# GpSimd's indexed stores of edge messages: ahead of each pair of units, one more wait, on a matmul group two units further on

## The chip, the cores and the metric

The kernel runs on one core of a Trainium2 chip. The metric is the device time of one execution in microseconds (us), as the median of several runs. The core has five engines with in-order instruction streams: TensorE (PE; its weight loads are listed as PEld), VectorE (DVE), ScalarE (ACT), GpSimd (POOL) and SyncE (SP, which here only issues transfers). They meet through semaphores.

## The reference

One layer of a graph network, added to its input: 12,500 nodes with 128 features, 400,000 edges sorted by their target node `dst`.

```python
h = relu(layernorm(x))                                  # 12500 x 128
hW = h @ W_in2f.T
Wij = smu(edge_attr_20 @ W_f1.T + b_f1) @ W_f2.T + b_f2 # per edge, 20 -> 128 -> 128
Wij = Wij * edge_weight[:, None]
x_ij = hW[dst] * Wij                                    # gather, times filter
agg = segment_sum(x_ij, src, num_segments=12500)        # src is not sorted
out = x + smu(agg @ W_o1.T + b_o1) @ W_o2.T + b_o2
```

`smu(x) = ((1 + a) x + (1 - a) x erf(mu (1 - a) x)) / 2` with a = 0.01 and mu = 2.5. The kernel computes it as a gelu plus a linear part.

## The kernel before, in words

**Units, pairs, rounds.** The edges are padded to 401,408 and cut into 784 units of 512 edges (4 tiles of 128). Two units share one load of edge attributes, of targets and of a window of `hW` rows (a pair, `PAIR`). The 784 units form ten rounds of 112, 112, 112, 112, 80, 80, 56, 40, 40 and 40 units (`SIZES`). All engines run the same sequence of beats (`beats`, line 394), one beat for each unit; in each round some beats are written out and the rest run in a hardware loop of four beats. In beat c an engine works on unit c and on unit c - 1.

**What a unit n needs.** In the order of the data:

- PE `filter1` (line 1202) writes the first filter layer into the one bank `p_z`; ACT `gelu_of` (line 700) and DVE `smu` (line 975) make `act1` from it.
- DVE `pick_target` (line 979) makes a one-hot matrix of targets; PE `targets` (line 1219, 12 matmuls) gathers `hW[dst]` into `p_h`; ACT `weigh` (line 711) scales it into `hg`.
- PE `filter2` (line 1208, 4 matmuls in f32, which the profile counts as 8) adds the second filter layer to `p_w[v]`, v = n % 2, in which ACT has first put the bias (`add_to_bias`, line 725). Its last matmul increments the semaphore `s_w`, so `s_w` reads n + 1 once unit n has its filter.
- DVE `bucket_of`, PE `rank` (lines 1225 and 1241) and DVE `places` (line 999) work out to which row of a bucket of source nodes each edge goes; DVE `row_numbers` (line 1010) writes the row numbers to `row_idx`.
- DVE `message` (line 992) multiplies `p_w[v]` by `hg` into one of four slots of `msg` (`RING = 4`) and increments `s_msg`.
- ACT `keys` (line 704) adds one column to the slot.
- POOL `scatter` (line 575) stores the slot to DRAM (`sorted_rows`) by four indexed transfers of 128 rows of 516 bytes (line 581). They increment `s_scat[slot]` by 16 each when they have landed.

**Who waits for the stores.** `keys`, `row_numbers` and `message` of unit n wait until the stores of unit n - 4 have landed, since they write to the same slot. At the first bucket of each next round SP waits for all stores of the round (`load_buckets`, line 485). One round later the rows come back bucket by bucket (`seg`), and DVE `bucket_hot` (line 1025), PE `bucket_sum` (line 1253) and DVE `gather_sum` (lines 1036 and 1038) add them to `agg`. After the last round the same steps run for its buckets, and then 28 groups of nodes go through the two output layers.

**The order on the engines around the change.** The order is written out by hand, in the `step` function of each engine. PE in beat c does `filter1(c)`, `bucket_sum`, `rank(c-1)`, `targets(c-1)`, `filter2(c-1)`. DVE does `bucket_hot`, `smu(c)`, `pick_target(c)`, `bucket_of(c)`, `places(c-1)`, `gather_sum`, `row_numbers(c-1)`, `message(c-1)`. ACT does `gelu_of(c)`, `weigh(c-1)`, `keys(c-1)`, `limits(c)`, `add_to_bias(c)`. POOL does nothing but `scatter(c-1)` in its beats:

```python
wait_for(pool, s_idx, n, 1, 1)
wait_for(pool, s_key, n, 1, 1)
wait_for(pool, s_msg, n, 1, 1)
```

and after them the four stores. `wait_for(eng, sem, n, 1, k)` waits until the semaphore is at least n + k; in a loop n is worked out from the loop's register. The real edges end with unit 781, so POOL issues 3125 stores. After them POOL adds a bias to 28 groups of nodes (`add_bias`, line 600).

Of the kernel before, what the change touches and what calls it, by code (L numbers as in the profile page):

```python
# [11 lines left out]
TILES_U = 4  # L12
# [65 lines left out]
def wait_for(eng, sem, at, times=1, plus=0):  # L78
    v = at.value(times, plus)
    if at.i is None and v <= 0:  # L80
        return
    eng.wait_ge(sem, v)


def build(nc, n_nodes, n_edges, n_real, F, R, t):
    n_units = n_edges // UNIT
# [20 lines left out]
    real_tiles = -(-n_real // LANES)  # L107
# [25 lines left out]
    with ctx:  # L133
# [6 lines left out]
        def sem(name):  # L140
            return ctx.enter_context(nc.semaphore(name))
# [67 lines left out]
        with ExitStack() as ahead_only:  # L209
# [66 lines left out]
        s_z, s_gelu, s_smu, s_w, s_pick, s_ph, s_hg, s_msg, s_key = (  # L276
            sem(n) for n in ("s_z", "s_gelu", "s_smu", "s_w", "s_pick", "s_ph", "s_hg", "s_msg", "s_key"))
# [116 lines left out]
        def beats(eng, step, tail=True):  # L394
            for rnd in range(rounds):
                for c in range(BODY * peel(rnd)):
                    step(Beat(rnd, None, c))
                if peel(rnd) < SIZES[rnd] // BODY:
                    with eng.Fori(peel(rnd), SIZES[rnd] // BODY) as i:
                        for c in range(BODY):  # L400
                            step(Beat(rnd, i, c))
            for c in range(SEG_LAG + n_groups + TAIL_MORE if tail else 1):
                step(Beat(rounds, None, c))
# [7 lines left out]
        def if_general(eng, program):  # L411
            eng.wait_ge(s_flag, 1)
            anywhere = eng.value_load(general[0:1, 0:1], min_val=0, max_val=1)
            with eng.If(anywhere):
                program()
# [131 lines left out]
        @block.gpsimd  # L547
        def _(pool):
            pool.memset(w_f1[:, :], 0.0).then_inc(s_pool, 1)
            pool.memset(attr[:, :, :], 1.0).then_inc(s_attr_ones, 1)  # L550
            pool.memset(before[:, :], 1.0)
            pool.memset(not_before[:, :], 1.0)
            pool.memset(step_rows[:, :], float(SPACE))
            pool.iota(lane[:, :], pattern=[[0, 1]], base=0, channel_multiplier=1,
                      allow_small_or_imprecise_dtypes=True)
            pool.iota(iota[:, :], pattern=[[1, NODE_P]], base=0, channel_multiplier=0,
                      allow_small_or_imprecise_dtypes=True)
            pool.iota(iota_bf[:, :], pattern=[[1, BUCKETS]], base=0, channel_multiplier=0,
                      allow_small_or_imprecise_dtypes=True)
            pool.iota(win_limit[:, :], pattern=[[H_GROUP, n_pairs]], base=H_GROUP * (H_AHEAD - H_LAND) - WINDOW, channel_multiplier=0,  # L560
                      allow_small_or_imprecise_dtypes=True)
            pool.iota(seed_row[:, :, :], pattern=[[buf_rows // SPACE, BUFS], [1, BUCKETS]], base=0, channel_multiplier=0,
                      allow_small_or_imprecise_dtypes=True)
            pool.memset(ident[:, :], 0.0)
            pool.memset(ident_bf[:, :], 0.0).then_inc(s_pool, 1)
            pool.wait_ge(s_pool, 2)
            for m in (ident, ident_bf):
                pool.affine_select(out=m[:, :], in_=m[:, :], compare_op=ALU.not_equal, fill=1.0, base=0,
                                   pattern=[[-1, LANES]], channel_multiplier=1).then_inc(s_pool, 1)
            pool.affine_select(out=before[:, :], in_=before[:, :], compare_op=ALU.is_gt, fill=0.0, base=0,  # L570
                               pattern=[[1, LANES]], channel_multiplier=-1).then_inc(s_pool2, 1)
            pool.affine_select(out=not_before[:, :], in_=not_before[:, :], compare_op=ALU.is_ge, fill=0.0, base=0,
                               pattern=[[-1, LANES]], channel_multiplier=1).then_inc(s_pool2, 1)

            def scatter(n, slot, tiles=TILES_U):
                wait_for(pool, s_idx, n, 1, 1)
                wait_for(pool, s_key, n, 1, 1)
                wait_for(pool, s_msg, n, 1, 1)
                pool.sem_inc(s_go, 1)
                for k in range(tiles):  # L580
                    pool.indirect_dma_start(out=sorted_rows[:, :],  # L581
                                            out_offset=bass.IndirectOffsetOnAxis(ap=row_idx[:, slot, k:k + 1], axis=0),
                                            in_=msg[:, slot, k, :], in_offset=None).then_inc(s_scat[slot], 16)

            def step(st):
                if st.opens(1) and st.has(1):
                    if 0 < st.rnd_of(1) < BUFS:
                        pool.wait_ge(s_zero[st.rnd_of(1)], 16 * BUCKETS)
                    if st.rnd_of(1) >= BUFS:
                        pool.wait_ge(s_seg, first_item[st.rnd_of(1) - BUFS + 1])  # L590
                if st.i is None and st.rnd == 0 and st.c == mid_step:
                    pool.wait_ge(s_zero[0], 16 * BUCKETS)
                if st.has(1):
                    n = st.at(1)
                    scatter(n, st.ring(1), TILES_U if n.i is not None else max(0, min(TILES_U, real_tiles - n.base * TILES_U)))

            def add_bias(g, turn):
                deep, times = g % DEEP, turn * (n_groups // DEEP) + g // DEEP + 1
                pool.wait_ge(s_xl[deep], 48 * times)
                pool.tensor_tensor(x_out[:, deep, :, :], x_out[:, deep, :, :], bias_o2[:, :].unsqueeze(1).to_broadcast([NODE_P, NODE_G, F]),  # L600
                                   ALU.add).then_inc(s_xb, 1)

            beats(pool, step, tail=False)
            for g in range(n_groups):
                add_bias(g, 0)

            def everywhere():
                rows = seg[:, :, :, :].rearrange("p a b c -> p (a b c)").bitcast(BF16)[:, 0:TILES_U * PARTS * F].rearrange(
                    "p (k f) -> p k f", k=TILES_U)
                pool.wait_ge(s_seg, first_item[rounds])  # L610
                with pool.Fori(0, n_units) as u:
                    pool.wait_ge(g_ld, u * 32 + 32)
                    pool.sem_inc(s_go, 1)
                    for k in range(TILES_U):
                        pool.indirect_dma_start(out=rows[:, k, :], out_offset=None, in_=h3[:, :],
                                                in_offset=bass.IndirectOffsetOnAxis(ap=g_dst[:, k:k + 1], axis=0),
                                                ).then_inc(g_win, 16)

                for g in range(n_groups):
                    add_bias(g, 1)  # L620

            if_general(pool, everywhere)
# [776 lines left out]
```

## Time and profile before

| what | value |
|---|---|
| time before, median of 3 runs | 4107.2 us (4103.52 to 4111.21) |
| span of the profiled execution | 5749.3 us |
| PE busy | 4327.1 us (75%), 32406 matmul records |
| DVE busy | 3410.0 us (59%) |
| ACT busy | 2118.5 us (37%) |
| POOL busy | 3038.4 us (53%), of it 2997.9 us for the 3125 stores |
| mean granted TensorE clock | 0.833 of full speed |
| HBM traffic | 128 GB/s over the span |

The profiled execution has no time of its own in the result beside its span, and its span is 1642.1 us, or 40%, longer than the median of the runs without a profile. So absolute times of the trace, and idle times above all, can't be set equal to those of a timed run; a duration of one instruction, or the spacing of instructions that follow each other without a wait, is the safer reading. "Idle before" in the tables is time in which an engine had nothing in execution, put down to what ended it; "remote" is a semaphore update whose source the profile doesn't tell, and "issue" is time for which it shows no wait at all.

### The profile page before, as it was taken

How to read it: one execution, taken by the hardware profiler on the slowest of the kernel's cores; microseconds unless marked ns; L12 is line 12 of the kernel's file. 1: busy time of each engine (PE TensorE's matmuls, PEld its weight loads, DVE VectorE, ACT ScalarE, POOL GpSimd, SP SyncE). 2: the span in 40 equal slices, each digit the busy share in tenths (PEclk: the TensorE clock that was granted, in tenths of full speed). 3: DMA queues.
4: the chain of work that ended last, by engine and by line, in shares of the span. 5: the costliest groups of instructions: out<-in, count | busy, mean ns of one | idle time of the engine just before them, and what ended most of it. 6: DMA issues, size and time to landing. Idle time of an engine off the chain costs nothing. (4 is left out here: it accounts for less than half of the span.)

```text
span 5749.3 us, 112809 instructions
## 1 busy us (share of the span) xinstructions
PE 4327.1 (75%) x32406; PEld 3547.2 (62%) x32406; DVE 3410.0 (59%) x11848; ACT 2118.5 (37%) x7302; POOL 3038.4 (53%) x3173
## 2 busy tenths in 40 slices
PE   5666557777777777777777777777777887877778
PEld 4455446666666666666666666666666666666567
DVE  6555445555565555565555666665555666666667
ACT  3455333333333333333333333333333333333333
POOL 4555555555555555555555555555555555555553
PEclk7777777887787788887887888898888988888989
DMA  6354434444443443444443444444444445554446
GB/s 171 110 134 134 113 111 131 129 135 125 131 123 113 114 115 110 117 115 112 112 115 109 118 134 135 136 140 121 123 124 124 143 143 140 146 144 129 128 134 191
DMA packets 459438, 737.76 MB, mean 128 GB/s; under 512 B 87025, under 2 KB 255323, under 8 KB 458961
## 3 DMA queue, kind: packets, MB, share of 16 engines
q1 hardware_dynamic: 291462, 461.44, 30.7%
q0 software_dynamic: 100000, 206.60, 10.7%
q10 hardware_dynamic: 67626, 65.48, 3.5%
q8 instruction: 168, 2.75, 0.2%
q14 instruction: 182, 1.48, 0.1%
HBM read 465.36 MB, written 267.82 MB: 128 GB/s over the span
## 5 line engine op out<-in xcount | busy, mean ns | idle before, releaser
L581 POOL DMA_INDIRECT sorted_rows<-msg,row_idx x3125 | 2997.9, 959 | 2627.5 <-DVE msg L992 1739.1
L711 ACT ACTIVATE hg<-p_h,weight 128x128 f32<-128x128 f32 x3136 | 894.7, 370 | 3102.5 <-remote 2804.8
L1253 PEld LDWEIGHTS p_seg<-seg_hot,seg 128*128 128x128 f32 x8288 | 1206.5, 213 | 784.6 <-issue 781.9
L999 DVE CUSTOM_DVE_ANT_0 product<-onehot,p_pos,start_at 128x112 bf16<-128x112 bf16 x3136 | 846.0, 324 | 1392.8 <-remote 1356.7
L1253 PE MATMUL p_seg<-seg_hot,seg 128*128 128x112 f32 x8288 | 1275.6, 298 | 337.3 <-issue 318.7
L1208 PE MATMUL p_w<-w_f,act 128*128 128x128 f32 x6272 | 1144.1, 327 | 223.2 <-issue 215.2
L1208 PEld LDWEIGHTS p_w<-w_f,act 128*128 128x128 f32 x6272 | 983.2, 233 | 240.2 <-issue 237.9
L1202 PE MATMUL p_z<-attr,w_f 128*128 128x512 f32 x1568 | 985.9, 707 | 186.0 <-issue 110.9
L1219 PE MATMUL p_h<-win,pick 128*128 128x128 bf16 x9408 | 826.9, 250 | 293.3 <-ACT hg L711 210.9
L992 DVE TENSOR_TENSOR msg<-p_w,hg 128x512 f32<-128x512 f32 x784 | 539.0, 688 | 736.0 <-ACT hg L711 448.8
L1219 PEld LDWEIGHTS p_h<-win,pick 128*128 128x128 bf16 x9408 | 700.7, 114 | 326.1 <-issue 319.8
L700 ACT ACTIVATE gelu<-p_z 128x512 f32<-128x512 f32 x784 | 473.8, 604 | 420.2 <-PE p_z L1202 161.4
L975 DVE SCALAR_TENSOR_TENSOR act<-p_z,gelu 128x512 f32<-128x512 f32 x784 | 536.3, 684 | 150.8 <-issue 114.2
L1025 DVE SCALAR_TENSOR_TENSOR seg_hot<-seg,p_iota 128x560 f32<-128x560 f32 (+2 forms) x700 | 580.7, 835 | 4.3 <-DMA seg<-sorted_rows 3.5
L1225 PE MATMUL p_pos<-onehot,not_before 128*128 128x112 bf16 x3136 | 333.6, 233 | 284.7 <-DVE place L999 149.1
L1225 PEld LDWEIGHTS p_pos<-onehot,not_before 128*128 128x128 bf16 x3136 | 254.3, 110 | 450.6 <-issue 438.5
L984 DVE TENSOR_TENSOR onehot<-p_iota,node_l 128x448 bf16<-128x448 f32 x784 | 479.3, 611 | 0.0
L725 ACT COPY p_w<-bias_f 128x512 f32<-128x512 f32 x784 | 477.9, 610 | 0.0
L1202 PEld LDWEIGHTS p_z<-attr,w_f 128*128 128x128 f32 x1568 | 292.3, 225 | 274.7 <-issue 200.3
L1241 PE MATMUL p_pos<-onehot,before 128*128 128x112 bf16 x3136 | 337.4, 236 | 50.1 <-issue 49.9
L979 DVE TENSOR_SCALAR pick<-ends,win_row 128x512 bf16<-128x512 uint16 x784 | 300.1, 383 | 0.0
L1241 PEld LDWEIGHTS p_pos<-onehot,before 128*128 128x128 bf16 x3136 | 232.2, 111 | 64.3 <-issue 64.1
(110 smaller groups left out, 1715.7 us busy)
## 6 DMA issues: line engine op xcount, KB each, us to landing
seg<-sorted_rows SPq DMA_DIRECT2D x448, 322.5 KB
seg<-sorted_rows SPq DMA_DIRECT2D x196, 516.0 KB
ends<-ends SPq DMA_DIRECT2D x392, 256.0 KB
sorted_rows<-msg,row_idx POOLq DMA_INDIRECT x3125
sorted_rows<-zero_rows ACTq DMA_DIRECT2D x336, 129.0 KB
win<-h SPq DMA_DIRECT2D x392, 96.0 KB
attr<-in_attrT SPq DMA_DIRECT2D x392, 80.0 KB
seg<-sorted_rows SPq DMA_DIRECT2D x56, 387.0 KB
```

Source lines behind the costliest of these rows:

```text
L581: pool.indirect_dma_start(out=sorted_rows[:, :], out_offset=bass.IndirectOffsetOnAxis(ap=row_idx[:, slot, k:k + 1], axis=0), in_=msg[:, sl ...
L711: last = act.activation(hg[:, v, k, :], p_h[:, k, :], ACT.Copy, scale=weight[:, bass.ds(n.value(TILES_U, k), 1)])
L975: dve.scalar_tensor_tensor(act1[:, v, :], p_z[:, :], SMU_L, gelu[:, v, :], ALU.mult, ALU.add).then_inc(s_smu, 1)
L992: dve.tensor_tensor(msg[:, slot, :, 0:F], p_w[v][:, :, :], hg[:, v, :, :], ALU.mult).then_inc(s_msg, 1)
L999: last = dve.tensor_tensor_reduce(out=product[:, k, :], in0=onehot[:, slot, k, :], in1=p_pos[:, 0:BUCKETS], scale=1.0, scalar=start_at[:, ...
L1025: dve.scalar_tensor_tensor(seg_hot[:, it.slot, 0:n, :], seg[:, it.slot, 0:n, F:F + 1].to_broadcast([LANES, n, NODE_P]), -float(LANES * (it ...
L1202: pe.matmul(p_z[:, :], w_f1[:, :], attr[:, q, v * UNIT:(v + 1) * UNIT], start=True, stop=True).then_inc(s_z, 1)
L1208: last = pe.matmul(p_w[v][:, k, :], act1[:, v, k * LANES:(k + 1) * LANES], w_f2[:, :], start=False, stop=(k == TILES_U - 1), skip_group_ch ...
L1219: last = pe.matmul(p_h[:, k, :], pick[:, v, k * LANES:(k + 1) * LANES], win[:, q, part * F:(part + 1) * F], start=(part == 0), stop=(part ...
L1225: last = pe.matmul(p_pos[:, 0:BUCKETS], not_before[:, :], onehot[:, slot, k, :], start=False, stop=False, skip_group_check=True)
L1241: last = pe.matmul(p_pos[:, 0:BUCKETS], before[:, :], onehot[:, slot, k, :], start=False, stop=False, skip_group_check=True)
L1253: last = pe.matmul(out, seg[:, it.slot, l * it.tiles + k, 0:F], seg_hot[:, it.slot, l * it.tiles + k, :], start=(k == 0), stop=(k == it.ti ...
```

## The change

`scatter` gets one more argument, `opens_pair`. It is true where n is even (`st.v(1) == 0`), that is for the first unit of each pair n, n + 1. There POOL first waits until `s_w` is at least n + 3, which is the end of `filter2` of unit n + 2; near the end of the edges the number is cut to the number of units, 784. The stores, their order, the semaphores that they increment and all other engines stay as they are.

```diff
-            def scatter(n, slot, tiles=TILES_U):
+            def scatter(n, slot, opens_pair, tiles=TILES_U):
+                if opens_pair:
+                    if n.i is None:
+                        pool.wait_ge(s_w, min(n_units, n.base + 3))
+                    else:
+                        wait_for(pool, s_w, n, 1, 3)
                 wait_for(pool, s_idx, n, 1, 1)
                 wait_for(pool, s_key, n, 1, 1)
                 wait_for(pool, s_msg, n, 1, 1)
...
-                    scatter(n, st.ring(1), TILES_U if n.i is not None else max(0, min(TILES_U, real_tiles - n.base * TILES_U)))
+                    scatter(n, st.ring(1), st.v(1) == 0, TILES_U if n.i is not None else max(0, min(TILES_U, real_tiles - n.base * TILES_U)))
```

How it stands on POOL at the first four units, before (`s_msg`, `s_idx` and `s_key` are counts of finished messages, row numbers and keys):

```order
L581 DMA sorted_rows<-msg,row_idx 258048x129 [waits s_msg,s_idx,s_key]
L581 DMA sorted_rows<-msg,row_idx 258048x129 x3
L581 DMA sorted_rows<-msg,row_idx 258048x129 [waits s_msg,s_idx,s_key]
L581 DMA sorted_rows<-msg,row_idx 258048x129 x3
L581 DMA sorted_rows<-msg,row_idx 258048x129 [waits s_msg,s_idx,s_key]
L581 DMA sorted_rows<-msg,row_idx 258048x129 x3
```

and now, the same place:

```order
L586 DMA sorted_rows<-msg,row_idx 258048x129 [waits s_msg,s_key,s_w,s_idx]
L586 DMA sorted_rows<-msg,row_idx 258048x129 x3
L586 DMA sorted_rows<-msg,row_idx 258048x129 [waits s_msg,s_idx,s_key]
L586 DMA sorted_rows<-msg,row_idx 258048x129 x3
L586 DMA sorted_rows<-msg,row_idx 258048x129 [waits s_msg,s_key,s_w,s_idx]
L586 DMA sorted_rows<-msg,row_idx 258048x129 x3
```

Units 0 and 2 wait for `s_w` as well; unit 1 follows unit 0 with the waits that it had. No row has moved on any engine.

In the loop of a round POOL's four beats now read as follows (the loop begins with the second unit of a pair; `L82` is `wait_ge`, `L399` the loop):

```order
L586 DMA sorted_rows<-msg,row_idx 258048x129 [waits s_msg,s_idx,s_key]
L586 DMA sorted_rows<-msg,row_idx 258048x129 x3
L82 REGISTER_ALU
L82 REGISTER_ALU [waits s_w]
L586 DMA sorted_rows<-msg,row_idx 258048x129 [waits s_msg,s_idx,s_key]
L586 DMA sorted_rows<-msg,row_idx 258048x129 x3
L82 REGISTER_ALU
L586 DMA sorted_rows<-msg,row_idx 258048x129 [waits s_msg,s_idx,s_key]
L586 DMA sorted_rows<-msg,row_idx 258048x129 x3
L82 REGISTER_ALU
L586 DMA sorted_rows<-msg,row_idx 258048x129 [waits s_msg,s_key,s_w,s_idx]
L586 DMA sorted_rows<-msg,row_idx 258048x129 x3
```

The second and the fourth unit of the loop body are those that open a pair.

## Rows read from the trace of the kernel before

**Rows 1.** The page: span, busy time of each engine, and granted clock in 40 slices.

```profile
span 5749.3 us, 112809 instructions
...
PE 4327.1 (75%) x32406; PEld 3547.2 (62%) x32406; DVE 3410.0 (59%) x11848; ACT 2118.5 (37%) x7302; POOL 3038.4 (53%) x3173
...
PEclk7777777887787788887887888898888988888989
```

**Rows 2.** Line 581 by itself, the stores: min/median/max in ns, first and last start.

```profile
L581 POOL DMA_INDIRECT sorted_rows<-msg,row_idx x3125: 952/958/1222, 28.4 to 5630.4; - x196
```

**Rows 3.** Timeline of POOL, 3009 to 3024 us: start, length, instruction [idle before].

```profile
3009.46 0.96 POOL L581 DMA_INDIRECT sorted_rows<-msg,row_idx  x1 [2.67 <-DVE msg L992]
3010.72 0.95 POOL L581 DMA_INDIRECT sorted_rows<-msg,row_idx  x1 [0.30 <-issue]
...
3018.30 0.96 POOL L581 DMA_INDIRECT sorted_rows<-msg,row_idx  x1 [0.30 <-issue]
3023.80 0.96 POOL L581 DMA_INDIRECT sorted_rows<-msg,row_idx  x1 [4.54 <-DVE msg L992]
```

**Rows 4.** Waits: who waited for whom, us in total, times, longest us.

```profile
ACT hg L711 <- remote: 2804.8, 378, 12.0
POOL sorted_rows L581 <- DVE msg L992: 1739.1, 482, 5.7
DVE product L999 <- remote: 1356.7, 306, 8.8
```

**Rows 5.** Timeline of PE, the same stretch; the last rows lie behind a full burst of stores.

```profile
3009.98 1.13 PE L1202 MATMUL p_z<-attr,w_f 128*128 128x512 f32 x2 [0.86 <-DVE act L975]
...
3013.10 1.11 PE L1208 MATMUL p_w<-w_f,act 128*128 128x128 f32 x8
3014.05 1.06 PE L1202 MATMUL p_z<-attr,w_f 128*128 128x512 f32 x2
...
3017.95 0.38 PE L1253 MATMUL p_seg<-seg_hot,seg 128*128 128x112 f32 x2 [1.06 <-issue]
3019.38 0.25 PE L1225 MATMUL p_pos<-onehot,not_before 128*128 128x112 bf16 x1 [1.05 <-issue]
```

**Rows 6.** Timeline of ACT and DVE, the same stretch.

```profile
3009.42 0.23 ACT L704 ACTIVATE msg<-node_p 128x4 f32 x1
3009.80 0.62 ACT L725 COPY p_w<-bias_f 128x512 f32<-128x512 f32 x1
3021.03 1.14 ACT L711 ACTIVATE hg<-p_h,weight 128x128 f32<-128x128 f32 x4 [9.29 <-remote]
...
3007.86 0.69 DVE L992 TENSOR_TENSOR msg<-p_w,hg 128x512 f32<-128x512 f32 x1 [3.36 <-remote]
3012.01 0.68 DVE L992 TENSOR_TENSOR msg<-p_w,hg 128x512 f32<-128x512 f32 x1
```

**Rows 7.** Windows: busy us of each engine between two messages, and in early and late rounds.

```profile
core 0: us, PE busy (x) PEld busy (x) DVE busy (x) ACT busy (x) POOL busy (x), PEclk, DMA share, GB/s
3007.86:3012.01 4.15, 3.29 (x25) 2.62 (x24) 4.12 (x16) 3.08 (x10) 1.94 (x3) 1.00 0.42 119
...
800.00:1200.00 400.00, 291.88 (x2110) 240.27 (x2111) 227.16 (x806) 142.98 (x504) 211.77 (x222) 0.79 0.46 128
3200.00:3600.00 400.00, 312.63 (x2424) 260.13 (x2423) 246.12 (x858) 141.78 (x501) 216.03 (x226) 0.88 0.45 131
```

**Rows 8.** Timeline of the start: stores of units 0 and 1, message 0, filter2 of units 0 to 2.

```profile
28.41 1.12 POOL L581 DMA_INDIRECT sorted_rows<-msg,row_idx  x1 [22.44 <-issue]
35.76 0.96 POOL L581 DMA_INDIRECT sorted_rows<-msg,row_idx  x1 [2.43 <-DVE msg L992]
...
26.65 0.69 DVE L992 TENSOR_TENSOR msg<-p_w,hg 128x512 f32<-128x512 f32 x1 [3.03 <-ACT hg L711]
...
19.16 2.05 PE L1208 MATMUL p_w<-w_f,act 128*128 128x128 f32 x8 [4.14 <-DVE act L975]
32.63 1.13 PE L1208 MATMUL p_w<-w_f,act 128*128 128x128 f32 x8
36.41 1.11 PE L1208 MATMUL p_w<-w_f,act 128*128 128x128 f32 x8
```

## The prediction

> **What bounds the kernel now.** I read the page first. No engine looks full: PE is busy for 75% of the span, DVE for 59%, POOL for 53% [rows 1]. But this span is 5749.3 us and the runs take 4107.2, so I don't read idle time off it; I look for what can't be shorter in a run without a profile.
>
> The line of the stores gives 3125 of them at a median of 958 ns [rows 2]. The timeline of POOL shows what they cost: where nothing holds them, eight in a row start at 3009.46 to 3018.30, seven steps in 8.84 us, 1.263 us each, 0.96 busy and 0.30 between [rows 3]. So the stores alone take 3124 x 1.263 + 0.96 = 3946.6 us. Before the first lie 28.4 us, and behind the end of the last (5631.4) 117.9 us of last buckets and output layers [rows 1, 2]. The sum is **4092.9 us**, and the median run takes 4107.2: 14.3 us are left for all pauses of POOL. I conclude that in a timed run **GpSimd issues stores nearly without a pause**, 5.05 us for each unit, and that the other engines keep ahead of it.
>
> Can they? In an undisturbed stretch one message follows the other after 4.15 us (3007.86 to 3012.01), with DVE busy for 4.12 of it at full clock [rows 6, 7], and PE comes from one first layer to the next in 4.07 us (3009.98 to 3014.05) [rows 5]. Both are under 5.05. They are held by the ring: `keys`, `row_numbers` and `message` of unit n wait for the stores of unit n - 4.
>
> The profiled execution behaves otherwise. POOL waits 482 times for a message, 1739.1 us in all, ACT 378 times before `hg` and DVE 306 times before `product`, both for something the profile can't name [rows 4]. In the stretch shown PE's `targets` is over before 3013.3, its `filter2` begins at 3013.10, and yet ACT starts `hg` only at 3021.03, after 9.29 us of idleness; meanwhile PE creeps, with pauses of 1.05 us inside a group of matmuls that waits for nothing [rows 5, 6]. The release comes 1.77 us after the end of a burst of eight stores (3019.26) [rows 3]. Whatever that is, at this size it can't be in the timed runs, which have 14 us for it, as long as the spacing of the stores is the same there. (The Trainium skill, page "NOTIFIC — the notification-queue block", section 7.1, says that the block which writes trace records never drops one inside but holds up its producers. That would put the pauses down to the recording; no run here shows it.)
>
> **The change, part by part.** No instruction of work is added, removed or moved; 392 waits on `s_w` are added on POOL, one for each pair. In the loops each adds a register instruction, which POOL's sequencer runs while a store is in execution; I cost it at nothing, with the 0.96 us of a store as its cover, and at most one such instruction per pair if it is not covered.
>
> Behind the waiting instruction stand only the eight stores of its pair and those of later ones. For the stores wait: message, keys and row numbers four units later, SP at the first bucket of each round (eight units behind the round's last), and the tail. The wait itself is for `filter2` of unit n + 2, which needs nothing of the stores of n or n + 1, so it can't lock.
>
> *The start.* Message 0 ends at 27.34, and the first store starts at 28.41. `filter2` of unit 2 ends at 36.41 + 1.11 = 37.52 [rows 8]. So the first pair starts 10.2 us later. Since POOL is what the whole kernel waits for, what it loses before it runs full is not made up: this is 10.2 us at the end. If POOL is short of work for some units in a timed run too, the last moment at which it is short decides instead, and there the shift is what lies between message n and `filter2` of n + 2 with engines running free: from 3008.55 to 3014.21, 5.7 us [rows 5, 6]. I take 8, between the two, as the recording shows POOL short of work at its start (7.35 us from unit 0 to unit 1 against 5.05) [rows 8] but can't tell how long that lasts without a recording. Both ends go into the range.
>
> *The steady state.* `filter2` of n + 2 hangs on the bias of n + 2, which on ACT stands behind `keys` of n + 1, which waits for the stores of n - 3. The last of these starts nine steps before the pair n would, 11.4 us, and has landed at most 0.96 + 1.77 us later, 8.6 us before the pair. From `keys` to the end of the bias it is 3009.42 to 3010.42, 1.0 us [rows 6], then `filter2`, 1.11 [rows 5]. So the semaphore is there some **6.5 us before** POOL gets to the pair, if PE has done its earlier groups. The wait costs nothing as long as this reserve holds. Before the change only the message of n had to be there, which waits for the stores of n - 4: their last starts thirteen steps ahead, 16.4 us, less 2.7 for length and landing and 0.7 for the message [rows 3, 6], a reserve of 13.0. So the change halves the reserve of the one engine that must not pause.
>
> *The end.* The last stores come 8 us later, and the tail with them.
>
> Sum: 4107.2 + 8 = **4115 us**. The recorded span has its long pauses ahead of most bursts, and there the added wait lies beside the message that POOL waits for anyway; I expect it within 1.5% of 5749.
>
> One rule of the Trainium skill speaks to the spacing itself. The row first: beside a DVE that is busy for 4.12 of 4.15 us the stores keep their 0.96 us, and over all 3125 the shortest and the longest are 952 and 1222 ns [rows 2, 3, 7]. The page "SBUF — State Buffer", section "SBUF: two separate sides", says that a DVE instruction in a two-port mode locks GpSimd out, so that it can't write the descriptors of its transfers. By that, when the stores run would matter, and 3125 x 0.26 us = 0.8 ms would be the most at stake; the trace doesn't agree that it happens here, and the sum stays.
>
> **The rivals.**
>
> *A, the forecast: full POOL, wait covered but at the start.* +5.7 to +10.2 us, 4113 to 4117. Chance 0.40. A difference of 0.2% (8.2 us) is about what a measurement of this kernel can tell from none, so half of this case falls on either side.
>
> *B, the reserve doesn't hold: slower by more.* The place is POOL at the head of a pair while PE is at its lower clock. The mean granted clock is 0.79 of full speed at 800 to 1200 us and 0.88 later [rows 7]; with two levels, 1.2 and 2.4 GHz, that is 42% of the time at the lower. `filter2` took 2.05 us at the start and 1.11 later [rows 8], a ratio of 1.85, so a unit of PE takes some 7.5 us there instead of 4.07 and falls 2.5 us behind the stores. The 6.5 us are gone after 2.6 units; from then on POOL pauses. It decides from stretches at the lower clock of over some 20 us, or from any stall of PE over 6.5 us. If one pair in three loses 0.5 us, it is 65 us more: 4180. For it: PE is idle a fifth of the time behind a full POOL, and idleness is what went with a lower clock. Against it: a PE that lags has no idleness. Chance 0.26.
>
> *C, the pauses of the recording are real, and the change orders them: faster.* Then the stores are closer together in a timed run than 1.263 us. At the least, with no gap between them, they take 3125 x 0.96 = 3000 us, and 961 us are pauses. The recording has 482 pauses for 391 pairs; the change would leave one for each pair and let PE hand over `filter2` of two further units before each burst. With 91 of 482 gone, 961 x 0.19 = 181 us: 3926. With the spacing of the trace it can't gain over 14.3 us: 4093. For it: in the stretch shown everything is released just behind a burst's end. Against it: the sum that comes out within 0.4% with full stores. Chance 0.16.
>
> *D, the change does nothing.* If POOL is not what the end waits for, stores that are two units late land before the ring needs them: eight stores and the landing are 11.9 us, four units at 5.05 are 20.2. 4107. Chance 0.18.
>
> **The numbers.** The likeliest is A, 4115. The range takes in A, D, C as far as the trace's spacing allows it (4093, with some margin) and B to 65 us over A: 4087 to 4188; what is left out is the far end of C and a worse B, some 0.15. Slower: half of A and B, 0.46. Same: half of A and D, 0.38. Faster: C, 0.16.
>
> **What would show it.** In the changed profile the first store should start near 38.6 instead of 28.4. POOL's waits should name PE's `filter2`, line 1208 moved by five, in place of the message. Bursts should begin at even units only. The spacing should stay at 1.263 us, and the recorded span within 1.5%. I am wrong if a timed run is faster by over 14 us: then the stores were never 1.263 us apart without a recording, or POOL was not what bounds. I am wrong the other way if it is slower by over 12 us: then the reserve of 6.5 us is not there, and a version that waits for `filter2` of n + 1 should give most of it back.

## The result, and the profile after

The changed kernel takes **4127.25 us** in the median of four runs (4126.2 to 4134.98). Four runs of the kernel before on the same chip have a median of 4105.36 us (4101.37 to 4111.21). The ratio is 1.0055, with a 95% interval of 1.0043 to 1.0066: **slower by 22 us**, where 8 were forecast.

The page of the changed kernel. First the lines that answer to [rows 1], then its chain by engine, then the line of the stores:

```profile
span 4126.0 us, 112900 instructions
...
PE 3554.0 (86%) x32406; PEld 2965.5 (72%) x32406; DVE 3387.0 (82%) x11848; ACT 2149.7 (52%) x7302; POOL 3044.7 (74%) x3173
...
PEclk9999999999999999999999999999999999999989
...
POOL 35%; issue 22%; DMA 20%; PE 11%; DVE 8%; ACT 2%; POOLq 1%; ACTq 1%; SPq 0%; DVEq 0%
...
L586 POOL DMA_INDIRECT sorted_rows<-msg,row_idx x3125 | 3003.7, 961 | 1002.4 <-issue 868.7
```

The first thing to see is the span. The profiled execution itself took 4127.92 us, 1.9 us more than its span and 0.7 us more than the median. So recording costs nothing that shows in this run, and the 5749.3 us of [rows 1] can hardly be its doing. The clock was granted at 0.97 of full speed, against 0.833 there. What the difference is, the second and third groups of runs tell.

The waits of the changed kernel (who waited for whom: us in total, times, longest us):

```profile
ACT msg L709 <- DMA sorted_rows<-msg,row_idx: 1279.6, 629, 8.4
POOL sorted_rows L586 <- issue: 868.7, 2845, 0.8
DVE row_idx L1015 <- DMA sorted_rows<-msg,row_idx: 554.5, 405, 7.2
...
POOL sorted_rows L586 <- PE p_w L1213: 51.7, 111, 6.8
POOL sorted_rows L586 <- ACT msg L709: 41.2, 36, 30.5
```

This is the picture that the prediction drew from the sum alone. ACT's `keys` and DVE's `row_numbers` wait for stores to land, so both are ahead of POOL, and POOL waits for almost nothing: 2845 of its idle times are the ordinary 0.3 us between two stores. Of the 1739.1 us on a message in [rows 4] 22.9 are left, and "remote" is gone. New is the 51.7 us on `filter2`; most of its 111 times are the ordinary 0.3 us, only put down to it.

The timeline of POOL at the start, which answers to [rows 8] (units 0 and 1, then the first stores of unit 2):

```profile
36.46 1.12 POOL L586 DMA_INDIRECT sorted_rows<-msg,row_idx  x1 [30.49 <-ACT msg L709]
37.88 0.96 POOL L586 DMA_INDIRECT sorted_rows<-msg,row_idx  x1 [0.30 <-DVE row_idx L1015]
39.15 0.95 POOL L586 DMA_INDIRECT sorted_rows<-msg,row_idx  x1 [0.30 <-issue]
...
45.45 0.95 POOL L586 DMA_INDIRECT sorted_rows<-msg,row_idx  x1 [0.30 <-issue]
52.55 0.95 POOL L586 DMA_INDIRECT sorted_rows<-msg,row_idx  x1 [6.14 <-PE p_w L1213]
```

The first store starts 8.05 us later than in [rows 8] (in two later profiles of the kernel before it starts at 27.05 and 27.92). The spacing of the stores is as before: seven steps take 45.45 - 36.46 - 0.16 (the first is 1.12 long) = 8.83 us, 1.26 each. But the second pair stands still for 6.14 us. Over the whole run the starts of the 3125 stores leave 26.2 us above a steady spacing of 1.263, counting what is over 0.1 us, and 17.8 of these lie ahead of seven pairs, released by `filter2`: 5.8 us at unit 2, 0.7 at 4, 0.9 each at 66 and 110, 1.6 at 222, 1.35 at 334, 6.5 at 662. Units 110, 222, 334 and 662 are the last pairs of four rounds (rounds begin at 112, 224, 336 and 664).

### The profile page after: what moved, and what is told of

It reads as the page before. It is cut to its first block, busy times and chain, and to the rows that moved or that the text cites. A ratio compares the mean times of both kernels' runs of the same rounds, so it can differ in the third digit from the quotient of the medians.

```text
span 4126.0 us, 112900 instructions
## 1 busy us (share of the span) xinstructions
PE 3554.0 (86%) x32406; PEld 2965.5 (72%) x32406; DVE 3387.0 (82%) x11848; ACT 2149.7 (52%) x7302; POOL 3044.7 (74%) x3173
## 4 chain that ended last, share of the span: by engine, by line
POOL 35%; issue 22%; DMA 20%; PE 11%; DVE 8%; ACT 2%; POOLq 1%; ACTq 1%; SPq 0%; DVEq 0%
POOL sorted_rows L586 35%; DMA sorted_rows<-msg,row_idx 18%; PE p_seg L1258 4%; PE p_w L1213 3%; PE p_z L1207 2%; DVE product L1004 2%; DVE msg L997 1%; DVE seg_hot L1030 1%; PE p_h L1224 1%; DVE act L980 1%; DVE onehot L989 1%; DVE pick L984 1%; ACT p_w L730 1%; PE p_w L1268 1%; DVE row_idx L1015 0%
## 5 line engine op out<-in xcount | busy, mean ns | idle before, releaser
L1258 PEld LDWEIGHTS p_seg<-seg_hot,seg 128*128 128x128 f32 x8288 | 1055.5, 196 | 330.6 <-issue 328.8
L1213 PE MATMUL p_w<-w_f,act 128*128 128x128 f32 x6272 | 902.6, 288 | 352.6 <-ACT p_w L730 345.4
L1213 PEld LDWEIGHTS p_w<-w_f,act 128*128 128x128 f32 x6272 | 783.1, 196 | 403.8 <-issue 401.0
L1258 PE MATMUL p_seg<-seg_hot,seg 128*128 128x112 f32 x8288 | 1047.1, 278 | 13.6 <-issue 13.6
L1207 PE MATMUL p_z<-attr,w_f 128*128 128x512 f32 x1568 | 890.6, 651 | 86.8 <-DVE act L980 59.9
L709 ACT ACTIVATE msg<-node_p 128x4 f32<-128x4 bf16 (+1 forms) x784 | 166.2, 212 | 1280.4 <-DMA sorted_rows<-msg,row_idx 1279.6
L1224 PE MATMUL p_h<-win,pick 128*128 128x128 bf16 x9408 | 660.3, 220 | 13.1 <-ACT hg L716 7.5
L1015 DVE TENSOR_TENSOR row_idx<-place,place_max 128x4 int32<-128x4 f32 x784 | 126.6, 162 | 564.4 <-DMA sorted_rows<-msg,row_idx 554.5
L1224 PEld LDWEIGHTS p_h<-win,pick 128*128 128x128 bf16 x9408 | 559.3, 99 | 16.2 <-issue 10.1
L1207 PEld LDWEIGHTS p_z<-attr,w_f 128*128 128x128 f32 x1568 | 244.5, 196 | 162.3 <-DVE act L980 101.8
```

The costliest lines, as they stand in the source:

```text
L1207: pe.matmul(p_z[:, :], w_f1[:, :], attr[:, q, v * UNIT:(v + 1) * UNIT], start=True, stop=True).then_inc(s_z, 1)
L1213: last = pe.matmul(p_w[v][:, k, :], act1[:, v, k * LANES:(k + 1) * LANES], w_f2[:, :], start=False, stop=(k == TILES_U - 1), skip_group_ch ...
L1224: last = pe.matmul(p_h[:, k, :], pick[:, v, k * LANES:(k + 1) * LANES], win[:, q, part * F:(part + 1) * F], start=(part == 0), stop=(part ...
L1258: last = pe.matmul(out, seg[:, it.slot, l * it.tiles + k, 0:F], seg_hot[:, it.slot, l * it.tiles + k, :], start=(k == 0), stop=(k == it.ti ...
```

## The experiments

Each comparison has its own runs of the kernel before on its own chip. They fell on chips of two kinds, and nothing below can be read without this: on some the kernel before takes 4105.36 to 4114.27 us (called **A** here), on others 5761.86 to 5871.56 (called **B**), always the same within one comparison. No chip was used for two comparisons, so that the two kinds belong to the chips, and not to the time at which they were used, is not shown. The result above is from A.

### Without the start, without the ends of rounds (a chip of kind B)

These were meant to show where the 22 us lie. `before_again` is the kernel before, for its profile.

> The kernel before, profiled again. Theory 1 (stores without a pause are what bounds; the pauses of the first recording were no part of a timed run): a span near 4100 us, first store at 28 us, pauses of POOL behind the first store of 15 us or less in all. Rival (the pauses belong to this kernel whenever it is recorded, and the added wait takes them away): a span near 5750 us again, with bursts of eight stores and 4.5 us between them.

`free_start` waits for no filter at the first two pairs:

```diff
-                if opens_pair:
+                if opens_pair and not (n.i is None and n.base < 4):
```

> The change without its wait ahead of the first two pairs. Theory 1 (of the 22 us, 8.1 are the later first store and 5.8 the pause ahead of unit 2, the rest are waits at the ends of rounds): 14 us less than the change, 4113 us, +0.2% against before. Rival (POOL is short of filters all along and the start is made up later): within 3 us of the change, 4125 us.

`free_ends` waits for none at the last pair of a round, where the filter is that of the next round's first unit:

```diff
-  scatter(n, st.ring(1), st.v(1) == 0, ...
+  scatter(n, st.ring(1), st.v(1) == 0 and (st.c != 3 if n.i is not None else n.base + 2 not in starts), ...
```

> The change without its wait ahead of the last pair of each round (in the rounds that are a hardware loop, without it ahead of every second pair, the last among them). Theory 1: the waits ahead of units 222, 334 and 662 go, 1.6 + 1.3 + 6.5 = 9.4 us, so 4118 us, +0.3%. Rival (a pause saved there is paid at the next pair, since PE is what is late): within 3 us of the change, 4125 us.

`free_both` has both edits.

> The change without either. Theory 1: the two savings add, 4104 us, within 0.1% of before, although over 200 of the 392 waits are still there. Rival (many small pauses of the remaining waits make up the loss): over 4113 us.

Measured: the kernel before 5871.56 us (nine runs, eight of them within 5862.59 to 5883.24, the ninth 6097.75 at a granted clock of 0.549); `free_start` 6288.63, ratio 1.0704 (1.0682 to 1.0727); `free_ends` 6177.02, 1.0521 (1.05 to 1.0542); `free_both` 6179.23, 1.0521 (1.0497 to 1.0545). The expectations for the three variants missed by some 2000 us, since they spoke of a kernel of 4105 us. The span of `before_again` is near that of its rival, but not for the rival's reason, as its time without a profile is the same. These runs can't settle where the 22 us lie; that `free_both` costs as much as `free_ends` says only that the wait at the start counts for nothing on B. They settle another question. `before_again` has a span of 5867.2 us and took 5869.09 with the profile, about the 5871.56 of the runs without one. These are its waits:

```profile
ACT hg L711 <- remote: 2965.3, 393, 10.0
POOL sorted_rows L581 <- DVE msg L992: 1832.3, 463, 5.4
DVE product L999 <- remote: 1442.2, 316, 6.6
```

They are the three of [rows 4] again, a little larger. So by its span, clock and waits the profile shown ahead of the prediction came from a chip of kind B, where the kernel before is really that slow. There is no profile of the kernel before on A. On B the wait costs 5% and more. POOL's waits for two of the variants:

```profile
POOL sorted_rows L586 <- PE p_w L1213: 1358.3, 231, 10.7
```

in `free_start`, and in `free_both`

```profile
POOL sorted_rows L586 <- PE p_w L1213: 965.3, 165, 7.9
```

The change itself was not timed on a chip of kind B; its nearest relatives cost 5.2 to 7.0% there.

### The wait alone at the start, and moved by one unit either way (a chip of kind A)

The kernel before took 4105.77 us (4102.47 to 4109.48, 21 runs) on this chip. `after_again` is the change once more.

> The change as it is, beside the kernel before on one chip. The first comparison stood on a chip on which the kernel before takes 4105 us (A); the first four experiments on one on which it takes 5872 (B), as the first profile did. On a chip like A: +0.55%, 4127 us, with pauses of POOL of 26 us behind the first store. On a chip like B, where PE's semaphores come late while stores run: theory 2 (a pair then starts only when two more filters are through, which stores held up, and each burst of eight has a longer pause ahead of it) +5 to +7%, 6170 to 6290 us, bursts of eight at even units. Rival (the change was made for that and orders the bursts): faster than before there.

Measured: 4129.95 us, ratio 1.0054 (1.0039 to 1.007), 24.2 us more than before, the first result again.

`only_start` keeps the wait at the first two pairs and nowhere else:

```diff
-                if opens_pair:
+                if opens_pair and n.i is None and n.base < 4:
```

> The added wait ahead of the first two pairs alone. On a chip like A, theory 1 (the later start is not made up, as POOL has no pauses left that could take it in): +14 us, 4119 us, +0.34%. Rival (the ring makes it up): within 4 us of before. On a chip like B POOL pauses all the time, so the start is made up: within 0.2% of before.

Measured: 4112.58 us (4110.91 to 4123.25), ratio 1.0017 (1.0008 to 1.0026), **6.8 us more** than before, half of the 14 expected. The start is then some 30% of the change's cost. Its POOL shows both pairs:

```profile
39.46 1.12 POOL L586 DMA_INDIRECT sorted_rows<-msg,row_idx  x1 [33.48 <-ACT msg L709]
...
54.66 1.02 POOL L586 DMA_INDIRECT sorted_rows<-msg,row_idx  x1 [5.21 <-PE p_w L1213]
```

The first store is later than the change's, the second pair stands still as well, and yet the end comes only 6.8 us later. Part of what is lost here is idle time that the kernel before has too: in [rows 8] it needs 7.35 us from unit 0 to unit 1, where stores without a pause need 5.05. What counts is the last unit for which POOL would be short of work without the added wait too. By the traces that is unit 5: its message ends at 61.95 us here, and `before_again` stores it 0.91 us behind the message (61.60 and 62.51). As an estimate it would have been stored at 62.9; with the wait it starts at 69.90, **7.0 us** later, close to the 6.8 measured.

`plus1` waits for `filter2` of unit n + 1, `plus3` for that of n + 3:

```diff
-                        pool.wait_ge(s_w, min(n_units, n.base + 3))
+                        pool.wait_ge(s_w, min(n_units, n.base + 2))   # plus1; plus3: n.base + 4
-                        wait_for(pool, s_w, n, 1, 3)
+                        wait_for(pool, s_w, n, 1, 2)                  # plus1; plus3: n, 1, 4
```

> The wait ahead of a pair n is for the second filter layer of n + 1 in place of n + 2. On a chip like A, theory 1 (reserve of 6.5 us becomes 11.6): first store some 5 us later than before, hardly a pause elsewhere, +5 to +10 us, 4110 to 4115 us. Rival (a POOL wait on PE costs something each time, whatever the reserve): as the change, 4127. On a chip like B, theory 2: the filter of n + 1 comes a unit earlier, so less than half of the loss of the change, +0 to +3%.

> The wait ahead of a pair n is for the second filter layer of n + 3. On a chip like A, theory 1: the reserve is 6.5 - 5.05 = 1.4 us, so POOL is late whenever PE is at its lower clock or a unit of it takes longer; between +1% and +8%, 4150 to 4430 us, and PE named ahead of most pairs. Rival (the reserve was far larger than worked out, PE runs ahead by units): under +1%. On a chip like B: slower than the change by more than its own loss.

Measured: `plus1` 4111.61 us (4108.75 to 4119.35), ratio 1.0014 (1.0005 to 1.0023), 5.8 us more than before; `plus3` **4635.05** us (4625.73 to 4635.75), ratio 1.128 (1.1263 to 1.1297), 529 us more. `plus1` came out at the time expected, `plus3` is above the 4430 us at which its expectation ended. One unit of distance less gives most of the change's 24.2 us back; one more costs twenty times as much. POOL's wait in `plus1` is put down by the profile as

```profile
POOL sorted_rows L586 <- PE p_w L1213: 27.7, 91, 0.3
```

where none is longer than the ordinary gap. But its one long pause is the added wait as well, under another name:

```profile
58.80 2.02 PE L1213 MATMUL p_w<-w_f,act 128*128 128x128 f32 x8
...
61.67 1.01 POOL L586 DMA_INDIRECT sorted_rows<-msg,row_idx  x1 [8.96 <-DVE msg L997]
```

The second row is the first store of unit 4, and the message named is that of unit 5, which this store doesn't need. What it needs is `filter2` of unit 5, the first row, which ends at 60.82; the store starts 0.85 us later, about what it takes behind any such wait. So the "hardly a pause elsewhere" of its expectation does not hold. By the estimate from message 5 (61.61 + 0.91, against 66.78 for unit 5) `plus1` loses 4.3 us there, of the 5.8 measured. In `plus3` the wait has the line

```profile
POOL sorted_rows L586 <- PE p_w L1213: 502.4, 282, 36.6
```

The pauses of `plus3` add up to 530.8 us, 1.36 us for each of 391 pairs. Against `only_start` that is 519.2 us more, and the first store starts 3.1 later: 522 us in all. The medians differ by 522.5, the spans of the two traces by 512.8. What POOL pauses is not made up later: it is what the end waits for.

**The ends of rounds**, from the traces of this chip. I take the twelve units around each of the nine round starts and subtract 48 x 1.263 us from what POOL needs for them. In `only_start`, which has no added wait there, 3.2 us are left over in all nine; in `plus1` 2.8; in `after_again` **15.1** (13.7 in the trace of the first result). So the change loses 11 to 12 us there. With the 6.8 of the start that is 18 or 19 of the 24.2 us of this chip. The remaining 5 or 6 are not placed: by the same sum the rest of the run, from unit 8 on and outside these stretches, stands 12.4 us above 1.263 a step in `after_again` and 14.1 in `only_start` (8 of each because the median spacing on this chip is 1.266), so the profiles show no loss there. They can't show it either: the profiled execution of `only_start` took 4123.25 us, 10.7 above the median of its eleven runs, that of `after_again` 4133.54, 3.6 above its own. The spans of the two traces differ by 10.6 us, the medians by 17.4. No kernel that leaves out the ends alone ran on A; the split rests on traces, good to some 7 us, not on a removal.

### One more instruction behind each unit's stores (B, then A)

The traces of kind B have something in common with [rows 3, 5, 6]. The instruction on PE is over, and the engine that waits for it goes on 2 to 10 us later, shortly behind the end of a burst of stores. I call an update of one of PE's semaphores late when it comes over 1 us behind the end of the instruction that makes it. In a second profile of the kernel before on another chip of kind B, `before_look`, 1910 of 3414 updates are late, and 869 of these come 1.5 to 1.8 us after the end of the last store of a burst. Of the updates that ACT and DVE make there 5 of 2886 and 8 of 3533 are late; of PE's in the changed kernel's trace on A, 5 of 3782. If it is the unbroken row of stores that holds them back, a short piece of other work on POOL between units should let them through earlier. `one_more_op` is the kernel **before** with a small memset behind every fourth store, and a wait for this memset ahead of the next unit's first:

```diff
+        idle_on = sb("idle_on", [LANES, 256])
+        s_extra = sem("s_extra")
...
+                wait_for(pool, s_extra, n)
...
+                pool.memset(idle_on[:, :], 0.0).then_inc(s_extra, 1)
```

> The kernel before, profiled on whichever chip this is. On a chip like A, theory 1: a span near 4104 us (so the recording costs nothing and the 5749 us of the first profile were the chip's), first store at 27 to 28 us, pauses of POOL behind it of 10 to 15 us in all, next to none at the ends of rounds. Rival (the recording lengthens this kernel everywhere): a span over 5700 us.

> The change without its waits ahead of the first two pairs and of the last pair of each round (in the loops, of every second pair). On a chip like A, theory 1 (the loss sits at the start, 7 us by the run with these waits alone, and at the ends of rounds, 8 to 10 us by the traces): within 3 us of before, 4103 to 4109 us. Rival (many small pauses at the other 200 waits): over 4113 us.

> The kernel before with one memset of 128x256 f32 on POOL behind each unit's stores. From the memsets of the trace (205 ns for 128 columns, 1805 ns for 2048) it takes 0.31 us. On a chip like A, theory 1 (POOL's stores bound the kernel, nothing hides there): +784 x 0.31 = +243 us at the least, +480 us if it also brings a gap of 0.30 like that between stores; 4350 to 4590 us. Rival (POOL has slack that the profile doesn't show): under +20 us. On a chip like B, where POOL pauses for 4.5 us ahead of each burst: under +2%, as it only splits bursts.

This chip is of kind B again, so `before_look` and `free_both_2` leave open what they were meant to show on A. Measured against 5761.86 us (5747.9 to 5767.83): `free_both_2` 6062.23, ratio 1.0523 (1.0505 to 1.0541), as on the other chip of this kind. `one_more_op` **5151.92** (5149.17 to 5157.44), ratio 0.8949 (0.8933 to 0.8965): 10.5% faster with 784 instructions more, where a change under 2% was expected. Its POOL in the middle of the run:

```profile
3005.95 0.96 POOL L584 DMA_INDIRECT sorted_rows<-msg,row_idx  x1 [0.31 <-issue]
3006.91 0.33 POOL L587 MEMSET idle_on<- 128x256 f32 x1
3008.08 0.97 POOL L584 DMA_INDIRECT sorted_rows<-msg,row_idx  x1 [0.84 <-POOL idle_on L587]
...
3011.89 0.96 POOL L584 DMA_INDIRECT sorted_rows<-msg,row_idx  x1 [0.31 <-issue]
3012.84 0.33 POOL L587 MEMSET idle_on<- 128x256 f32 x1
3014.04 0.97 POOL L584 DMA_INDIRECT sorted_rows<-msg,row_idx  x1 [0.86 <-DVE msg L996]
```

The gap between two units is now 1.17 us instead of 0.30: 0.33 for the memset and 0.84 for the wait on its semaphore. And POOL's waits for a message shrink from 1754.4 us in `before_look` to this:

```profile
POOL sorted_rows L584 <- DVE msg L996: 410.4, 202, 3.6
```

Late updates are not fewer, 2460 by the same count, but they are late by 3.3 us in the median instead of 5.0, and 1450 of them arrive 0.6 to 0.9 us after the end of a memset. Whether it takes the memset or only the pause between stores, no run separates. Does the same help on A, where nothing is late? `pairs_and_op` is the change with the same memset:

> The change and one memset of 128x256 f32 on POOL behind each unit's stores, which puts 1.17 us between the stores of two units instead of 0.30 (as the trace of the run before this shows it). On a chip like A, theory 1 (the issue of stores bounds the kernel, nothing hides there): 784 x 0.87 = +682 us on the change's 4128, so 4810 us, +17% against before, with no wait on PE that counts. Rival (POOL had slack): under +5%. On a chip like B, theory 2 (PE's semaphores get through only where POOL stops issuing stores for about a microsecond; the memset makes such a stop in each unit): faster than before there by 7 to 10.5%, and the wait ahead of pairs costs under 4% of the memset version's 0.895. Rival (the added wait costs 5% or more on B whatever the stores do): a ratio over 0.94.

Measured against 4114.27 us (4112.27 to 4117.33): **4884.9** (4881.58 to 4886.84), ratio 1.187 (1.1854 to 1.1886), 771 us more, and 75 us over the 4810 expected. The timeline again shows the memset and the 0.84 us behind it:

```profile
3004.01 0.33 POOL L592 MEMSET idle_on<- 128x256 f32 x1
3005.18 0.97 POOL L589 DMA_INDIRECT sorted_rows<-msg,row_idx  x1 [0.84 <-POOL idle_on L592]
```

784 times the 0.87 us of the longer gap are 682 us. The stores' starts leave 788.7 us above a spacing of 1.263: 719.3 ahead of units, and 69.4 between the stores of one unit, 0.03 each, which the expectation had at nothing. The changed kernel's trace has 29.0 by the same sum, 759.7 less, and its span is 758.3 us shorter. On A nothing hides what POOL loses. A version that beats the kernel before on both kinds was not found: the one edit helps on B by 610 us and, as far as `pairs_and_op` tells, costs some 750 on A (771 less the change's own 22).

## Why the prediction was right, and its size wrong

**What bounds: right.** "GpSimd issues stores nearly without a pause" holds on A: `plus3` and `pairs_and_op` lose in time what POOL's pauses add, 522 and 760 us, within some 10. The spacing of 1.263 us and the lengths stayed (952, 958 and 1478 ns as shortest, median and longest, against [rows 2]; only the longest is new). That the sum came within 14.3 us of the time is in part luck, as its rows are from a chip of kind B: behind the last store the changed kernel needs 114.0 us on A, not 117.9, and on the chip of `after_again` the median spacing is 1.266 us, 9 us more over 3124 steps.

**The start: right in size.** Forecast 5.7 to 10.2 us, taken as 8; the wait at the first two pairs alone gives 6.8. The first store was expected near 38.6 and came at 36.46. Of the prediction's two cases the one with 5.7 us has the mechanism: "the last moment at which it is short decides", which by the estimate above is unit 5, with 7.0 us. The 8 lay between a case that holds and one that doesn't. Not foreseen was that the *second* pair pauses as well. It waits for `filter2` of unit 4, which starts 9.9 us after the end of that of unit 3:

```profile
38.67 1.11 PE L1213 MATMUL p_w<-w_f,act 128*128 128x128 f32 x8
...
48.43 1.46 PE L1224 MATMUL p_h<-win,pick 128*128 128x128 bf16 x12 [3.13 <-DMA win<-h]
49.68 2.02 PE L1213 MATMUL p_w<-w_f,act 128*128 128x128 f32 x8
```

PE stood idle several times in between, last for 3.13 us until a window of `hW` had been loaded. The clock adds only 0.9 us: the filter of unit 3 ran at 2.4 GHz (granted clock 1.00 from 38.6 to 39.8 us), that of unit 4 at 1.2 GHz (0.50 from 49.6 to 51.7).

**The steady state: here the size failed.** The step was "the semaphore is there some 6.5 us before POOL gets to the pair", made of "landed at most 0.96 + 1.77 us later" and 1.0 + 1.11 us from `keys` to the end of `filter2`. The changed kernel's trace gives the reserve itself. For each pair I take the time from the end of `filter2` of n + 2 to the moment when POOL could start the pair, 0.30 us behind the last store of unit n - 1: the median is **4.4 us**, and one pair in twenty has 1.8 or less. A pair in the middle of the run, unit 586 (`keys` of 587, `filter2` of 588; its own first store starts at 3018.31):

```profile
3006.95 0.96 POOL L586 DMA_INDIRECT sorted_rows<-msg,row_idx  x1 [0.30 <-issue]
...
3009.26 0.21 ACT L709 ACTIVATE msg<-node_p 128x4 f32<-128x4 bf16 x1 [0.18 <-DMA sorted_rows<-msg,row_idx]
...
3012.39 1.11 PE L1213 MATMUL p_w<-w_f,act 128*128 128x128 f32 x8
```

The last store of unit 583 ends at 3007.91, `keys` of 587 starts 1.35 us later, and `filter2` of 588 ends at 3013.50: 4.24 us after `keys`, not 2.1, because PE first had `bucket_sum`, `rank` and `targets` to do. "If PE has done its earlier groups" was a condition, and it often isn't met: over the pairs the median is 2.5 us, but a quarter take 3.7 or more. The larger miss is the other term, the landing: over all units `keys` starts 3.1 us in the median after the end of the stores that it waits for. The prediction took 1.77 for an upper bound, from one place of [rows 3, 6]. That was no landing but the time from a burst's end to `hg` on ACT, which waits for PE, on a chip of kind B.

The prediction had named this outcome: slower by over 12 us would mean that "the reserve of 6.5 us is not there", and the version with n + 1 should give most of it back. It was 22 us, and `plus1` gives back 18.4 of 24.2. The measured time lies outside the 4113 to 4117 of the forecast A, and inside the stated range because that took in rival B.

The same measure for `filter2` of n + 3 has a median of -0.7 us: a unit less is 5.05 us less. A store starts 0.84 us after the filter that released it. Together that is 1.5 us late on each pair, and `plus3` lost 1.36.

**The ends of rounds: not priced.** A reserve of 4.4 us holds on an ordinary pair and not on all. The worst is unit 662. The rows are those of ACT, PE and POOL in this order:

```profile
3397.62 0.21 ACT L709 ACTIVATE msg<-node_p 128x4 f32<-128x4 bf16 x1 [8.44 <-DMA sorted_rows<-msg,row_idx]
...
3398.74 2.04 PE L1213 MATMUL p_w<-w_f,act 128*128 128x128 f32 x8 [6.09 <-ACT p_w L730]
3400.58 2.02 PE L1207 MATMUL p_z<-attr,w_f 128*128 128x512 f32 x2
3402.39 2.07 PE L1258 MATMUL p_seg<-seg_hot,seg 128*128 128x112 f32 x16
...
3405.86 0.22 PE L1241 MATMUL p_pos<-seeds,step_rows 128*128 128x112 bf16 x1 [1.21 <-DVE counts L1022]
...
3406.79 1.11 PE L1213 MATMUL p_w<-w_f,act 128*128 128x128 f32 x8
...
3408.74 0.96 POOL L586 DMA_INDIRECT sorted_rows<-msg,row_idx  x1 [6.84 <-PE p_w L1213]
```

`keys` of unit 662 waits 8.44 us for the stores of 658 to land, 10.9 us after their last one has ended. PE waits 6.09 us for the bias behind it and comes back at 1.2 GHz: 2.04 us for the filter of unit 663, 2.02 for `filter1`. A round's first unit then has a step of its own, a matmul that needs `counts` from DVE (1.21 us idle), ahead of the filter of 664. The kernel before would have stored 662 when its message was there; the change makes POOL wait for all of this. `only_start`, without the wait there, shows it: the filter of 664 is as late, at 3409.62, but the stores of 662 start at 3404.49, 0.30 us behind the one before them. That is rival B's mechanism, in a few places instead of one pair in three: 11 or 12 us and not 65. Why the landing took so long there is open. Transfers of 516 KB into `seg` run in that stretch, but no run separates them.

**The reading of the first profile: wrong.** "The recorded span within 1.5%" of 5749 came out as 4126.0. The prediction put 1642 us down to the recording. By the runs the recording costs next to nothing: 5867.2 us of span and 5869.09 with the profile against a median of 5871.56 on B, 4126.0 and 4127.92 against 4127.25 on A; the most that any profiled execution stands above its median is the 10.7 us of `only_start` on A and 22.6 of `free_both` on B. The Trainium skill's page "NOTIFIC — the notification-queue block", section 7.1, offered a mechanism for a longer recording; no run here shows it. The pauses of [rows 4] are real times of a chip of kind B. The forecast survived because the sum was built from lengths and spacings only, which are nearly the same on both. Rival C took those pauses for real and expected the change to order them and gain. They are real, but on B the kernels with the added wait are 5 to 7% slower, not faster; in `free_start` POOL waits 1358.3 us for `filter2`, a release that comes late as the others do: 388 of 779 updates of its semaphore are late, by 7.2 us in the median.

What stays open: what differs between the two kinds of chip, and by which way an unbroken row of stores holds up PE's semaphore updates on one of them. The runs show when the updates arrive, and that they arrive sooner with a memset and a wait for it between units; they don't show where they are held up.

## What to carry to other kernels

When the span of a profile and the timed runs differ by 40%, compare the profiled execution's own time with runs without a profile on the same chip before blaming the recording. On an engine that must not pause, a wait is priced by its reserve at the worst places (start, ends of rounds, a late landing), and every instruction ahead of the awaited one on its own engine belongs to the sum. A sweep of the wait's distance by one unit either way measures the reserve: here 5.8, 24 and 529 us for n + 1, n + 2 and n + 3. A profile that puts a pause down to one engine can name the wrong one of two semaphores that came close together: look for what ended 0.84 us earlier.

## What was not expected of the hardware

- The same kernel takes 4105 to 4114 us on some chips and 5762 to 5872 on others, at granted clocks of 0.97 and of 0.82 to 0.84, with nearly the same lengths and spacing of the stores. On the slower kind waits on PE's work end 2 to 10 us late while stores are issued without a break.
- On such a chip one memset of 0.33 us for every four stores, with a wait for it, made the kernel 10.5% faster.
- A store that waits for an instruction that has just ended starts 0.84 us behind it, be it a memset on POOL itself or `filter2` on PE (334 pairs of `plus3`: 0.81 to 0.99 us, median 0.84); a store behind a store has 0.30 us.
